# Mixture's weights fetched and split during attention's last batch, refinement's normalisations on ScalarE, and attention's jobs laid over 44 ticks

## What is computed

```python
x = x + layernorm(attention(layernorm(x)))        # 8 batches of 1024 rows, D = 256, 16 heads, causal
x = x + layernorm(ffn(layernorm(x)))
# attention: latent c_q = x W_DQ, c_kv = x W_DKV; Q = [c_q W_UQ, rope(c_q W_QR)],
#            K = [c_kv W_UK, rope(x W_KR)], V = c_kv W_UV; clip(scores, -80, 80), softmax, W_O
# ffn, twice: ctx = [integrated, v]
#   shared expert and the top 2 of 8 experts: gelu(ctx @ w1 + b1) @ w2 + b2 -> (a, b, g)
#   v_next = sigmoid(a) * v - softplus(b) * (x - mu); x_next = x + 0.1 * sigmoid(g) * v_next
#   integrated, v move towards the mixed result by halt = sigmoid(gelu(...) @ halt_w2 + halt_b2)
# out = xf + integration_weight * (gelu(integrated @ refine_w1 + b1) @ refine_w2 + b2)
```

## Time and profile before

| | us |
|---|---|
| median of 3 runs | 2999.1 (2995.45 to 2999.13) |
| the profiled execution | 3002.68 |
| its span | 3001.0 |
| PE busy | 2602.1 (87%) |
| DVE busy | 2386.0 (80%) |
| ACT busy | 1868.1 (62%) |
| POOL busy | 642.7 (21%) |

### The profile page before, as it was taken

The page is one execution under the profiler, slowest core; times in us unless marked ns, Lnnn a source line. Parts: engine busy times, 40 slices in busy tenths (PEclk is TensorE's granted clock), DMA queues, the critical chain, the costliest instruction groups (busy, mean ns, idle before and its releaser), DMA issues. The chain is left out here.

```text
span 3001.0 us, 42994 instructions
## 1 busy us (share of the span) xinstructions
PE 2602.1 (87%) x16008; PEld 1808.0 (60%) x16008; DVE 2386.0 (80%) x4031; ACT 1868.1 (62%) x2947; POOL 642.7 (21%) x441
## 2 busy tenths in 40 slices
PE   3888888888888971799999999999999999997986
PEld 2233333333333321688888888888888888886875
DVE  4577777767777664879888999889889898876998
ACT  1676766767676750666666766667666676664332
POOL 2013121111202010211212112121121221112666
PEclk8798989989998985999999999999999999998998
DMA  3451525435251503000000000000000000003231
GB/s 103 82 86 60 85 82 90 82 72 89 64 89 53 89 29 89 1 1 15 15 15 1 15 15 15 15 1 15 15 15 15 1 15 8 8 8 117 85 105 56
DMA packets 125681, 136.28 MB, mean 45 GB/s; under 512 B 17394, under 2 KB 105714, under 8 KB 125476
## 3 DMA queue, kind: packets, MB, share of 16 engines
q1 hardware_dynamic: 125476, 133.54, 19.3%
HBM read 87.10 MB, written 46.40 MB: 44 GB/s over the span
## 5 line engine op out<-in xcount | busy, mean ns | idle before, releaser
L385 ACT ACTIVATE probs<-psum_a 128x1024 f32<-128x1024 f32 (+3 forms) x768 | 601.0, 816 | 317.6 <-PE psum_a L654 313.6
L1418 PE MATMUL psum_f<-w,picked 128*128 128x256 f32 (+1 forms) x2304 | 721.6, 346 | 0.0
L1417 PE MATMUL psum_f<-w,picked 128*128 128x256 f32 x2304 | 620.5, 286 | 1.2 <-DVE picked L1240 1.2
L1418 PEld LDWEIGHTS psum_f<-w,picked 128*128 128x128 f32 x2304 | 445.8, 193 | 56.3
L461 DVE TENSOR_SCALAR probs<-probs 128x2048 f32<-128x2048 f32 (+3 forms) x320 | 303.8, 949 | 184.3 <-ACT probs L385 184.2
L1417 PEld LDWEIGHTS psum_f<-w,picked 128*128 128x128 f32 x2304 | 446.6, 194 | 1.5 <-DVE picked L1240 1.5
L654 PE MATMUL psum_a<-q_stack,k_stack 72*128 72x512 f16 (+3 forms) x1536 | 393.9, 347 | 38.1 <-ACT probs L385 17.6
L669 PE MATMUL psum_a<-probs,v 128*17 128x512 f32 (+3 forms) x3072 | 341.3, 518 | 1.8 <-DVE probs L461 1.7
L1049 ACT ACTIVATE gates<-psum_f 128x256 f32<-128x256 f32 (+1 forms) x384 | 185.9, 486 | 239.0 <-PE psum_f L1418 237.3
L1240 DVE TENSOR_TENSOR picked<-hid,masks 128x512 fp32r<-128x512 f32 x512 | 322.9, 690 | 14.2 <-PE psum_f L1418 11.2
L654 PEld LDWEIGHTS psum_a<-q_stack,k_stack 72*128 72x128 f16 x1536 | 99.8, 100 | 381.4 <-ACT probs L385 217.9
(11 more groups left out here) (282 smaller groups left out, 5558.0 us busy)
## 6 DMA issues: line engine op xcount, KB each, us to landing
heads_scratch<-kq_parts SPq DMA_DIRECT2D x64, 256.0 KB
k_stack<-heads_scratch SPq DMA_DIRECT2D x96, 128.0 KB
q_stack<-heads_scratch SPq DMA_DIRECT2D x96, 128.0 KB
x_in<-x_dram SPq DMA_DIRECT2D x8, 1024.0 KB, 5.4
x_res<-x_dram SPq DMA_DIRECT2D x16, 512.0 KB, 4.8
x_scratch<-y SPq DMA_DIRECT2D x16, 512.0 KB, 3.1
xs<-x_scratch SPq DMA_DIRECT2D x16, 512.0 KB, 3.8
xf_scratch<-xs SPq DMA_DIRECT2D x16, 512.0 KB, 2.9
```

The costliest lines, as they stand in the source:

```text
L385: act.activation(probs[:, s % PROB_SETS, 2 * u:2 * u + 2, q0:512], psum[:, 2 * u:2 * u + 2, q0:512], ACT.Exp, scale=exp_scale).then_inc(ex ...
L1417: pe.matmul(soft_out, x, cols[:, 1], start=start, stop=stop)
L1418: return pe.matmul(gate_out, x, cols[:, 2] if it == 0 else cols[:, 0::2], start=start, stop=stop)
```

## The change

One launch as before; what is computed does not change.

- A class `Late` holds mixture's weights for the whole launch. In one memory area lie, one after the other in time, attention's early buffers (x, projections' operands and weights; `place`) and then the raw and split weights. When the last projection of the last batch is done, POOL clears a few rows, SP issues the weights' loads (behind the last batch's stacks), and DVE splits them in ten steps, one in each of the ticks 24 to 33 of the last batch, each waiting for the one before.
- Mixture starts without loads of weights and without splitting; its mu matmuls use the two parts of the weights instead of the raw ones (24 calls, not 12). The identity matrix is loaded once.
- The job tables run over ticks 0 to 43 with a free tick after most pairs; output statistics move to ticks 9 and 34; POOL's order in a batch is changed to suit; `x_moments` moves from 37 to 38.
- In refinement ACT makes `base` and `scale` (Identity with a scale and a bias for each row), DVE adds the bias that POOL added and makes the shifts, and the store of a block comes one block later.

```diff
-    PROJECTION = {3: ("XT", 0, 0), 4: ("XT", 0, 1), 7: ("KR", 0, 0), 8: ("LAT", 0, 0), 11: ("QR", 0, 0), 12: ("QR", 0, 1),
-                  13: ("KH", 0, 0), 14: ("KH", 0, 1), 15: ("QH", 0, 0), 16: ("QH", 0, 1), 19: ("V", 0, 0), 20: ("V", 0, 1),
-                  21: ("XT", 1, 0), 22: ("XT", 1, 1), 24: ("KR", 1, 0), 25: ("LAT", 1, 0), 28: ("QR", 1, 0), 29: ("QR", 1, 1),
-                  30: ("KH", 1, 0), 31: ("KH", 1, 1), 32: ("QH", 1, 0), 33: ("QH", 1, 1), 34: ("V", 1, 0), 35: ("V", 1, 1)}
-    OUTPUT = {1: ("OT", 0, 0), 2: ("OT", 0, 1), 5: ("OR", 0, 0), 6: ("OR", 0, 1),
-              9: ("OT", 1, 0), 10: ("OT", 1, 1), 17: ("OR", 1, 0), 18: ("OR", 1, 1)}
+    PROJECTION = {3: ("XT", 0, 0), 4: ("XT", 0, 1), 8: ("KR", 0, 0), 9: ("LAT", 0, 0), 14: ("QR", 0, 0), 15: ("QR", 0, 1),
+                  17: ("KH", 0, 0), 18: ("KH", 0, 1), 20: ("QH", 0, 0), 21: ("QH", 0, 1), 23: ("V", 0, 0), 24: ("V", 0, 1),
+                  25: ("XT", 1, 0), 26: ("XT", 1, 1), 28: ("KR", 1, 0), 29: ("LAT", 1, 0), 33: ("QR", 1, 0), 34: ("QR", 1, 1),
+                  36: ("KH", 1, 0), 37: ("KH", 1, 1), 39: ("QH", 1, 0), 40: ("QH", 1, 1), 42: ("V", 1, 0), 43: ("V", 1, 1)}
+    OUTPUT = {0: ("OT", 0, 0), 1: ("OT", 0, 1), 6: ("OR", 0, 0), 7: ("OR", 0, 1),
+              11: ("OT", 1, 0), 12: ("OT", 1, 1), 31: ("OR", 1, 0), 32: ("OR", 1, 1)}
...
# SP, end of attention's batch loop
-            sp.wait_ge(x1_stored, 16 * 2 * BATCH)
+                if after == BATCH - 1:
+                    sp.wait_ge(late_cleared, 1)
+                    for dst, src in late_loads:
+                        sp.dma_start(dst, src).then_inc(late_in, 16)
...
# POOL, order in a batch
+                if 0 <= after < BATCH:
+                    k_rope(after, 1)
                 if 0 <= before:
                     y_scale(before, 1)
+                if 0 <= after < BATCH:
+                    q_rope(after, 1)
+                if 0 <= before:
                     add_residual(before, 1)
-                if 0 <= after < BATCH:
-                    k_rope(after, 1)
-                    q_rope(after, 1)
...
# DVE in attention
+            def split_late(step):
...
+                if step == 1:
+                    last = dve.tensor_copy(w1[:, 0], raw_w1[:, 1])
+                if step == 2:
+                    last = dve.tensor_copy(w2[:, 0], raw_w2[:, 1])
...
+                if step == 9:
+                    dve.tensor_copy(ws2[0:S_ROWS, 1], raw_s2[0:S_ROWS, 1])
+                    last = dve.tensor_tensor(w2[:, 1], raw_w2[:, 1], w2[:, 0].bitcast(F32), ALU.subtract)
+                last.then_inc(late.split, 1)
...
+                if w == BATCH - 1 and 24 <= t < 24 + late.SPLITS:
+                    split_late(t - 24)
...
-                    for half, first in ((0, 8), (1, 20)):
+                    for half, first in ((0, 9), (1, 34)):
...
-                    if t == 37:
+                    if t == 38:
                         x_moments(w + 2)
...
# mixture
+            sp.wait_ge(late.x1_stored, 16 * XS)
             for k in range(XS):
                 sp.dma_start(xs[:, k], blk_v[k]).then_inc(x_loaded[k], 16)
-            sp.wait_ge(cleared, 1)
-            for dst, src in loads:
-                sp.dma_start(dst, src).then_inc(weights_in, 16)
...
             x_row_stats(0)
+            first_values()
             x_normalize(0)
...
# refine, ACT
+            def base(k):
...
+                for t in range(BT):
+                    last = act.activation(y[:, k % BUFS, t, :], x1[:, k % BUFS, t, :], ACT.Identity, scale=rstd[:, k, t:t + 1],
+                                          bias=shift[:, k, t:t + 1])
+                last.then_inc(base_ready, 1)
+
+            def scale(k):
...
+                for t in range(BT):
+                    last = act.activation(y[:, k % BUFS, t, :], y[:, k % BUFS, t, :], ACT.Identity, scale=y_rstd[:, k % 2, t:t + 1],
+                                          bias=y_shift[:, k % 2, t:t + 1])
+                last.then_inc(scaled, 1)
...
# refine, DVE
+            def add_bias(k):
...
+                dve.tensor_tensor(y[:, k % BUFS], y[:, k % BUFS], bf2[:].unsqueeze(1).to_broadcast([P, BT, D]),
+                                  ALU.add).then_inc(biased, 1)
...
-                if 0 <= k < BLOCKS:
-                    base(k)
+                if 0 <= k < BLOCKS:
+                    add_bias(k)
                 if k >= 2:
-                    scale(k - 2)
-                if k >= 1:
+                    y_shifts(k - 2)
+                if 1 <= k <= BLOCKS:
                     add_refined(k - 1)
```

More of the change, by code:

```diff
@@ L39, in attention @@
+def attention(nc, late, x_dram, consts_dram, w_dram, late_dram, x1_dram):
     dh, dr, heads = HEAD, ROPE_DIM, HEADS
@@ L178, in attention @@
         x_res_loaded = sem("x_res_loaded")
-        x1_stored = sem("x1_stored")
+        x1_stored = late.x1_stored
+        late_cleared = sem("late_cleared")
+        late_in = sem("late_in")
+        late_loads = late.loads(late_dram, consts_dram, late_raw)
         block = ctx.enter_context(nc.Block())
@@ L996, in _ @@
             act.wait_ge(cleared, 1)
-            act.wait_ge(weights_in, 16 * len(loads))
+            act.wait_ge(late.split, late.SPLITS)
             act.activation(share[:, 1:2], share[:, 0:1], ACT.Tanh, scale=0.5).then_inc(share_tanh, 1)
@@ L1079, in _ @@
         def _(dve):
-            dve.wait_ge(weights_in, 16 * len(loads))
+            dve.wait_ge(late.split, late.SPLITS)
             split = [0]
@@ L1336, in _ @@
         def _(pe):
-            pe.wait_ge(weights_in, 16 * len(loads))
+            pe.wait_ge(late.split, late.SPLITS)
             for m in range(6):
                 for c in range(2):
-                    w = raw_w1[c][:, P * m:P * m + P] if m < 5 else raw_r1[:, c]
-                    last = pe.matmul(psum[0:w.shape[1], 0, m:m + 1], w, mu_col[:, c:c + 1], start=(c == 0), stop=(c == 1))
+                    for part in range(2):
+                        w = w1[:, part, c, P * m:P * m + P] if m < 5 else wr1[:, part, c]
+                        last = pe.matmul(psum[0:w.shape[1], 0, m:m + 1], w.bitcast(F32), mu_col[:, c:c + 1],
+                                         start=(c == 0 and part == 0), stop=(c == 1 and part == 1))
             last.then_inc(mu_part, 1)
@@ L1594, in _ @@
             act.wait_ge(weights_ready, 1)
[L1595 to L1605 removed]
+            def base(k):
+                act.wait_ge(x1_loaded[k % BUFS], 16 * (k // BUFS + 1))
+                if k >= BUFS:
+                    act.wait_ge(stored[k % BUFS], 16 * (k // BUFS))
+                for t in range(BT):
+                    last = act.activation(y[:, k % BUFS, t, :], x1[:, k % BUFS, t, :], ACT.Identity, scale=rstd[:, k, t:t + 1],
+                                          bias=shift[:, k, t:t + 1])
+                last.then_inc(base_ready, 1)
@@ new lines, in scale @@
+            def scale(k):
+                act.wait_ge(shift_ready, k + 1)
+                for t in range(BT):
+                    last = act.activation(y[:, k % BUFS, t, :], y[:, k % BUFS, t, :], ACT.Identity, scale=y_rstd[:, k % 2, t:t + 1],
+                                          bias=y_shift[:, k % 2, t:t + 1])
+                last.then_inc(scaled, 1)
+            for k in range(-1, BLOCKS + 2):
+                if k + 1 < BLOCKS:
+                    for c in range(2):
+                        job_ready(act, ("XT", k + 1, c))
+                        act.activation(ctx_t[:, (k + 1) % 2, 0, c], bank(("XT", k + 1, c)), ACT.Copy, scale=-1.0).then_inc(act_read, 1)
+                if 0 <= k < BLOCKS:
+                    base(k)
+                    for m in range(MC):
+                        job_ready(act, ("H", k, m))
+                        if MC * k + m >= 2:
+                            act.wait_ge(lower_made, MC * k + m - 1)
+                        act.activation(gel[:, m % 2], bank(("H", k, m)), ACT.Gelu, bias=bf1[:, m:m + 1])
+                        act.activation(hid[:, k % 2, 0, m], bank(("H", k, m)), ACT.Gelu, bias=bf1[:, m:m + 1]).then_inc(act_read, 1)
+                if k >= 2:
+                    scale(k - 2)
@@ L1625, in _ @@
             dve.wait_ge(mu_part, 1)
+            dve.scalar_tensor_tensor(out=shift[:], in0=mean, scalar=-1.0, in1=rstd, op0=ALU.mult, op1=ALU.mult)
             after(dve.tensor_tensor(bf1[:], bf1[:], psum[:, 0, 0:MC], ALU.add))
@@ L1785 @@
     out = nc.dram_tensor("out", (TOKENS, D), F32, kind="ExternalOutput").ap()
-    attention(nc, x, consts, attn_w, x1)
-    feed_forward(nc, x1, consts, ffn_w, xf, out)
+    with ExitStack() as ctx:
+        late = Late(nc, ctx)
+        attention(nc, late, x, consts, attn_w, ffn_w, x1)
+        feed_forward(nc, late, x1, consts, ffn_w, xf, out)
     r = run(nc, [arrays], core_ids=[0])
```

359 lines of the change are left out of this document (186 added, 173 removed).

## The result

| | before | after |
|---|---|---|
| median, us | 2999.1 (2995.45 to 3000.3, 4 runs) | 2943.2 (2941.64 to 2944.89, 4 runs) |
| ratio | | 0.9818, interval 0.9804 to 0.9833 |
| span of the profiled execution | 3001.0 | 2943.0 |

The change saves 56 us; the forecast was 130, and its range ended at 2922. Two of its four parts, the gap and refinement, came out near what was reckoned, and attention went the other way.

A forecast was written before the change was run, and what follows sets the result against it. Attention's middle batches had every engine below 90%; refinement's ten blocks were vector-bound. Terms -52 + 3 - 2 - 36 + 6 - 49 = -130 on 3002.7 gave 2872.7, less 3.6: 2869 us, range 2815 to 2922.

The forecast's parts named there:

- Part 1: Between attention and mixture: no waiting for weights or splitting, mu matmuls doubled; 52 us saved, bounds 49 to 57.
- Part 4: Refinement: matrix engine becomes the bound, ten blocks save 35 us, the end 13.6; 49 us saved, bounds 38 and 51.
- rival C: Refinement: ScalarE table loads make 14 us a block, 15 us saved instead of 35; near 2892 us, chance 0.04.
- Part 3: Attention's jobs over 44 ticks: middle batches at 127 us, 6 us saved in each of six, 36 in all.
- a free tick after two: Attention's job tables: no job needs a bank being read in the same tick, so waits like the 2.2 us go.
- 4 for waits I can't name: Middle attention batches: an allowance of 4 us per boundary for unidentified waits.
- 3 us of hold: Attention, tick 40: GpSimd's residual addition delays x's power, holding the vector engine 3 us ahead of its QH readings.
- The wait for the stacks: Tick 0 of the next attention batch: the first score waits for stack loads; 8 us per boundary with the hold's delay.
- rival A: Attention: relaying pays in full, no hold at tick 40 and no echo, batches at 117 us; near 2809, chance 0.17.
- the clean prices: Middle attention batches: 89 us for 48 jobless ticks plus 20 for the jobs without waits, 109 us.
- Rival B: Attention: relaying pays nothing, and late weights hold the vector engine 8 us at tick 24; 2917 us, chance 0.16.
- Part 2: Last attention batch: splits add about 21 us of vector work, some 11 on the path, bounds 4 and 16.

The follow-up runs named there:

- h: The kernel before with the new refinement alone; 2951.5 us, 0.9845.
- d: The changed kernel with half 0's output normalisation at tick 16, not 13; 2885.5 us, 0.9631.
- e: On top of d: half 1's normalisation at tick 44, not 38, x's power ahead of GpSimd's residual addition, half 1's store behind the first stack loads; 2866.3 us, 0.9556.
- j: On top of e: nine of the first head group's twelve stack loads no longer wait for the last QH write; 2829.3 us, 0.9421.
- i: On top of f: the last batch's weight splits from tick 28, not 24; 2885.4 us, 0.9615.
- b: The kernel before with the new job tables and orders alone; 3019.1 us, 1.0078.
- f: On top of d: batch 6's residual load issued ahead of the 54 late weight loads; 2879.1 us, 0.9602.

## Why the prediction was wrong

*Part 1, the gap: right.* 52 forecast, 52.9 measured, with the mu matmuls ending it. The load of x1 landed 4.9 us after its issue, inside its bounds. The upper bound of 57 was a slip: it took the load alone, and the same paragraph has the mu matmuls end at 52 at the soonest.

*Part 4, refinement: right, and 6 us too large.* 49 forecast, 46.3 measured for all behind the gap, 43 of it in refinement itself (h: 44) and 3 in mixture, which varies by more than that. No table load (rival C), 12.0 us a block, so the ten blocks gave the 35 forecast; the start and the end gave 8 where the end alone was to give 13.6. ScalarE took 9.8 us a block, for 8.9 by the sum.

*Part 3, the layout: wrong, and the step is the sentence that a free tick after two does away with waits as in the earlier trace rows.* It looked at which jobs share a bank, and not at what else DVE does in the tick in which it reads. QR of tick 15 follows OT of 12, with one free tick between, and that tick holds half 0's normalisation. The kernel before had the same: in front of the reading that the earlier trace rows waits for, DVE normalised half 0, and in front of the next reading an instruction was held by GpSimd's addition (rows in the last section). The forecast read the wait of the earlier trace rows as one of two jobs too close together alone, and the new layout kept what else stood in front of the reading. "4 for waits I can't name" was the term that stood for this; it was 9 (137.0 to 127.8 in d), of which about 5 are the wait and 4 the clock behind it. "3 us of hold" at tick 40 was the right place with a wrong cause and too small: the hold came from half 1's normalisation and an instruction held by GpSimd's addition, not from x's power behind it, and took 6 us out of ticks 39 to 43, 4 of which were to be had (127.8 to 123.8, e). The wait for the stacks was forecast at 8 and was 7.0 in the mean; taking most of it away gave 6.2 (j). With these gone a batch takes 117.6. That this is rival A's 117 is luck: A's 117 are the clean prices, 109, and 8 for the stacks, and in j only 1.9 are left of those. So the clean prices were some 7 us too low, which the forecast's other terms had no room for. 4 to 5 of the 7 lie in ticks 39 to 47 (24.7 us in j, of which 1.9 wait for the stacks; 18.3 by the forecast's prices); by what, no run shows. In one sum: 109 and 7, 9 at tick 15, 4 at tick 40 and 8 for the stacks (6.2 and the 1.9 left) make the 137 measured. How much the late normalisation and the earlier stack loads would give in the old layout, no run shows; so what the new tables themselves are worth stays open.

The range failed with it. The upper bound of a batch, 135, was exceeded by 2 us in the mean, since it took a larger hold at tick 40 and none anywhere else. Rival B had two of the four losses, the stacks and the late weights at tick 24 (8 us, 7.1 measured), and ended at 2917, because its loss from relaying stopped at zero.

*Part 2, the splits: the sum near, the cover wrong.* 107 forecast for the last batch, 116.4 measured, 108.6 in i by the same measure, where the wait is gone. In that, two misses cancel: without splits the new layout's last batch took 99.9 (b) for 96, and the splits cost 8.7 in i for 11. I had the loads begin 8 us into the batch and take 29 us, by before's spacing; they began at 11.8 and took 42.5, behind the 48 stack loads. The prediction said that without its 7 us of cover the wait goes to DVE one for one; DVE waited 7.1, and from f to i, where a wait of 7.6 went, the last batch lost 7.0.

The misses in one sum: six batches 60.6 (24.6 for -36), last batch 8.7, refinement 2.7, batch 0 1.7, prologue -0.8, gap -0.9: 72.0, from -130 to -58.

## What to carry to other kernels

When jobs are moved on a schedule of ticks, write down for each tick all that the reading engine does in it, and for each job which of those things stand in front of the reading it waits for; put long vector work that nobody waits for behind the readings, not in front. GpSimd's large addition held one vector instruction each time it stood beside attention's ticks, so place such a pair where nobody queues behind it; three ticks' difference for one normalisation was worth 58 us here. And a chain through DRAM should be cut at its last input: what doesn't depend on that input can go ahead of it.

## What the runs showed of the hardware

Beside GpSimd's addition over 1024 columns one DVE instruction between operands in SBUF is held, and ends 0.03 to 1.1 us behind the addition. All 14 additions that stood beside attention's ticks in the kernel after did this. It was so in the kernel before too, and PE waited behind it; DVE, GpSimd and PE there:

```profile
504.12 0.72 DVE L548 TENSOR_SCALAR y<-y,y_mean,y_rstd 128x256 f32<-128x256 f32 x2
504.77 0.68 DVE L457 SCALAR_TENSOR_TENSOR probs<-probs,tri 128x512 f32<-128x512 f32 x1
505.37 0.94 DVE L461 TENSOR_SCALAR probs<-probs 128x1536 f32<-128x1536 f32 x1
506.24 0.68 DVE L494 TENSOR_TENSOR rope_a<-psum_a,cos 128x512 f32<-128x512 f32 x1
506.84 2.25 DVE L457 SCALAR_TENSOR_TENSOR probs<-probs,tri 128x512 f32<-128x512 f32 x1
...
504.99 3.55 POOL L310 TENSOR_TENSOR y<-y,x_res 128x1024 f32<-128x1024 f32 x1 [1.27 <-DVE y L548]
...
510.34 0.79 PE L622 MATMUL psum_a<-latent_t,w_kv 128*128 128x512 f32 x1 [1.60 <-DVE rope_b L494]
```

The first row is the end of half 0's normalisation, and the fourth is the reading that the earlier trace rows waits for. The held instruction, 0.68 us by itself (second row), ends at 509.09, the addition at 508.54, and PE waits 1.6 us for the reading behind it.

The reading at 506.24 lies beside the addition as well and keeps its 0.68 us: it reads PSUM, as did three readings beside each of d's first additions (501.09, 0.68 us, for one), none of which was held.

The addition's own row grows too. It is 2.34 and 2.36 us long where no DVE instruction is under way, in the gap of the kernel before, 2.3 to 3.6 in the kernel after and 3.5 to 5.7 beside attention's ticks in the kernel before, for the same 1024 columns; so the mean of the earlier trace rows holds waiting. In the rows above, the instructions at 504.77 and 505.37 are not held though the addition's row has begun, which fits an addition that waits for them first (3.55 us for 2.34). Even an instruction over 8 columns is held in full (0.16 becomes 2.23).
By the Trainium skill, "SBUF — State Buffer", SBUF: two separate sides, GpSimd shares one pair of ports to SBUF with DVE instructions that run in a two-port mode or read two operands from SBUF, under an exclusive lock, which whoever comes first keeps for its whole instruction. The trace agrees for the addition, and with the readings of PSUM that went on beside it. GpSimd's power over 8 columns shows less: it lasted 2.03 us from 588.41, for 1.02 over 4 columns where DVE stood still, and DVE's clips over 512 columns beside it took their usual 0.42 and 0.67; how much of its row is waiting no run here took apart.

PE's clock fell to half after an idle of 4.2 us and came back 17 us later, so that a wait at tick 15 cost nearly its length again in the four ticks behind it; at full clock in d the same five ticks took 12.0 us for 21.8.
